# Reordering TensorE's step, and VectorE's and ScalarE's within a tile, in the first layer of a two-layer graph attention kernel

## What is computed

```python
enh = node_features + 0.1 * query_emb[None, :]
Q = (enh @ Wq + bq).reshape(N, H, D); K = ...; V = ...      # H = 4 heads of D = 64
rel = rel_w[edge_relations]                                 # 64 kinds of edge
mod_k = K[src] + 0.2 * rel[:, None, :]
scores = jnp.einsum('ehd,ehd->eh', Q[dst], mod_k) / D ** 0.5
ex = jnp.exp(scores - segment_max(scores, dst)[dst])
w = ex / segment_sum(ex, dst)[dst]
agg = segment_sum(w[:, :, None] * V[src], dst)
out = where(deg > 0, agg, V).reshape(N, H * D) @ Wo + bo
x = layernorm(out + node_features) * gamma + beta
```

## Time and profile before

| | |
|---|---|
| time, median of 3 runs | 4821.75 us (4820.29 to 4824.06) |
| the profiled execution | 4847.24 us, span 4845.9 us |
| PE busy | 4004.0 us, 83% |
| PEld busy | 2592.5 us, 53% |
| DVE busy | 3436.6 us, 71% |
| ACT busy | 2781.9 us, 57% |
| POOL busy | 3127.0 us, 65% |

### The profile page before, as it was taken

One profiled execution on the slowest core, in us unless ns is written; L12 is line 12 of the kernel. 1 busy time (PEld: TensorE's weight loads), 2 busy tenths in 40 slices (PEclk: granted clock), 3 DMA queues, 4 the chain that ended last, 5 costly groups with the idle time before them and its releaser, 6 DMA issues. The chain is left out here.

```text
span 4845.9 us, 149801 instructions
## 1 busy us (share of the span) xinstructions
PE 4004.0 (83%) x42462; PEld 2592.5 (53%) x42462; DVE 3436.6 (71%) x11602; ACT 2781.9 (57%) x7985; POOL 3127.0 (65%) x3229
## 2 busy tenths in 40 slices
PE   6978889889998888988889688777788777777785
PEld 4645545555555555555555456555565555555553
DVE  3235667677777777777777568888887787777887
ACT  2324444445454455445545367777777777777775
POOL 1226666666666666666666277777777777777773
PEclk9989999999999999999999677877767887888776
DMA  6878888888888888888888377777777777777774
GB/s 207 282 225 232 236 224 226 231 236 234 235 243 231 234 240 241 231 240 239 232 237 237 101 193 208 206 207 206 208 208 205 207 207 204 204 203 206 205 205 131
DMA packets 820558, 1052.06 MB, mean 217 GB/s; under 512 B 458633, under 2 KB 632338, under 8 KB 820464
## 3 DMA queue, kind: packets, MB, share of 16 engines
q0 software_dynamic: 225072, 726.83, 51.5%
q1 hardware_dynamic: 594078, 323.35, 26.7%
q10 hardware_dynamic: 1314, 0.99, 0.1%
HBM read 915.79 MB, written 133.39 MB: 217 GB/s over the span
## 5 line engine op out<-in xcount | busy, mean ns | idle before, releaser
L765 POOL DMA_INDIRECT typed_rows<-kv,typed_index x1563 | 1491.3, 954 | 857.4 <-PE typed_p_o L889 420.3
L1288 POOL DMA_INDIRECT plain_rows<-xp,plain_index x1563 | 1563.2, 1000 | 556.3 <-issue 437.2
L1140 ACT ACTIVATE typed_far<-typed_match,all_cst 128x416 bf16<-128x416 uint8 x521 | 334.2, 642 | 1002.2 <-DVE typed_col L991 983.8
L1393 PE MATMUL plain_p_o<-plain_rows,plain_weight_t 128*64 128x130 f32 (+1 forms) x8336 | 864.3, 350 | 49.5 <-DVE plain_weight_t L1419 48.8
L1380 PE MATMUL plain_p_s<-all_cst,plain_rows 128*128 128x128 f32 (+1 forms) x2084 | 453.9, 317 | 362.0 <-DMA plain_rows<-xp,plain_index 360.2
L1393 PEld LDWEIGHTS plain_p_o<-plain_rows,plain_weight_t 128*64 128x64 f32 (+1 forms) x8336 | 574.2, 170 | 212.0 <-issue 131.7
L851 PE MATMUL typed_p_kt<-all_cst,typed_rows 128*128 128x128 f32 x3126 | 473.8, 290 | 255.8 <-DMA typed_rows<-kv,typed_index 254.9
L964 DVE TENSOR_TENSOR typed_kt<-typed_p_kt,typed_rel 128x768 f32<-128x768 f32 x521 | 497.0, 954 | 230.7 <-PE typed_p_kt L851 202.2
L1380 PEld LDWEIGHTS plain_p_s<-all_cst,plain_rows 128*128 128x128 f32 (+1 forms) x2084 | 334.9, 173 | 515.1 <-issue 497.4
L851 PEld LDWEIGHTS typed_p_kt<-all_cst,typed_rows 128*128 128x128 f32 x3126 | 345.1, 145 | 359.1 <-DMA typed_rows<-kv,typed_index 299.0
L1426 DVE CUSTOM_DVE_ANT_0 plain_alpha<-plain_alpha,plain_far 128x416 f32<-128x416 f32 x521 | 310.6, 596 | 313.1 <-ACT plain_alpha L1542 299.9
(11 more groups left out here) (190 smaller groups left out, 6341.7 us busy)
## 6 DMA issues: line engine op xcount, KB each, us to landing
typed_match<-match SPq DMA_DIRECT2D x131, 208.0 KB
plain_match<-match SPq DMA_DIRECT2D x131, 208.0 KB
agg<-qkv_zero SPq DMA_DIRECT2D x98, 264.0 KB
typed_agg<-agg SPq DMA_DIRECT2D x98, 264.0 KB
plain_agg<-agg SPq DMA_DIRECT2D x98, 264.0 KB
kv<-qkv_kv SPq DMA_DIRECT2D x98, 258.0 KB
typed_kinds<-match SPq DMA_DIRECT2D x131, 192.0 KB
typed_rows<-kv,typed_index POOLq DMA_INDIRECT x1563
```

What stands on the lines that cost most here:

```text
L765: pool.indirect_dma_start(rows[:, r, j, :], None, k.kv, bass.IndirectOffsetOnAxis(ap=index[:, g, at:at + 1], axis=0)).then_inc(rows_in[r], 16)
L1140: act.activation(far[:], match[:, slab, t.slot(TPB)], ACT.Square, bias=cst[:, C_CODE:C_CODE + 1], scale=FAR).then_inc(far_ready, 1)
L1288: pool.indirect_dma_start(rows[:, r, j, :], None, k.xp, bass.IndirectOffsetOnAxis(ap=index[:, g, at:at + 1], axis=0)).then_inc(rows_in[r], 16)
L1393: last = pe.matmul(p_o[at:at + HC, t.slot(2), 0:2 * V], weight_t[0:e, t.slot(2), j * P + at:j * P + at + HC], val[:, 2 * V * g:2 * V * g + ...
```

## The change

TensorE's step gets another order, and VectorE's and ScalarE's lists get the same one. No instruction, wait, lag or buffer is added or removed.

- TensorE: from relations, keys, turned weights, scores, sums to turned weights, sums, scores, relations, keys. A block's update keeps its place ahead of the step, and the wait for `message_t_ready` stays with the sums, which are now second in the step.
- VectorE: from keys, weight copy, kinds, scores to weight copy, scores, kinds, keys, and the block pieces behind them as before.
- ScalarE: from message, relations, weight copy, mask, exponential, sums to message, weight copy, sums, exponential, relations, mask, and the block pieces behind them as before.

```diff
@@ attend_typed, TensorE
-            parts = (TilePart(0, relate), TilePart(KEY, arrive), TilePart(TURN_LAG, turn_weights), TilePart(SCORE, score))
-
             def step(t, copied=None):
-                for part in parts:
+                for part in (TilePart(TURN_LAG, turn_weights), TilePart(LAG, lambda b: aggregate(b, copied)), TilePart(SCORE, score),
+                             TilePart(0, relate), TilePart(KEY, arrive)):
                     part.at(t)
-                TilePart(LAG, lambda b: aggregate(b, copied)).at(t)
@@ attend_typed, VectorE
-            interleave(v, FIRST, TilePart(KEY + 2, add_keys), TilePart(TURN_LAG + 2, copy_weights), TilePart(0, prepare), TilePart(SCORE + 2, lower_bound),
+            interleave(v, FIRST, TilePart(TURN_LAG + 2, copy_weights), TilePart(SCORE + 2, lower_bound), TilePart(0, prepare), TilePart(KEY + 2, add_keys),
                        BlockPart(3, 8, end_norm), BlockPart(3, 5, normalize), BlockPart(6, 5, vary), BlockPart(4, 2, sum_up), BlockPart(5, 0, join),
@@ attend_typed, ScalarE
-            interleave(act, FIRST, BlockPart(2, 1, copy_message), TilePart(1, copy_relations), TilePart(TURN_LAG + 1, copy_weights), TilePart(SCORE, set_apart), TilePart(SCORE + 1, weigh), TilePart(LAG + 1, put),
+            interleave(act, FIRST, BlockPart(2, 1, copy_message), TilePart(TURN_LAG + 1, copy_weights), TilePart(LAG + 1, put), TilePart(SCORE + 1, weigh), TilePart(1, copy_relations), TilePart(SCORE, set_apart),
```

## The result

The changed kernel takes 4646.93 us (median), the kernel before 4822.91: a ratio of 0.9633, 95% interval 0.9617 to 0.9650. It saves 176 us where 109 were forecast (4713 us, range 4640 to 4840). One execution of the changed kernel took 5218.17 us at a granted clock of 0.625, where its others have 0.875 to 0.890, and the ratio leaves it out.

What follows compares the result with a forecast made beforehand. TensorE and POOL were taken to wait for each other through eight row buffers. Per 16 tiles 34.5 + 18.7 + 13.5 + 0.6 + 0.6 = 67.9 against 71.4 us, 109 us saved over 31.25 periods: 4713 us, range 4640 to 4840.

Steps and rivals of the forecast that it cites:

- The loop through the eight buffers: Sums free a row buffer, POOL refills it, keys need it: 9.73 us needed, 7.91 allowed; 7.5 us per period goes.
- The residue of 0.6: Row waits of TensorE left after the change, between 0 and 7.5 us per 16 tiles, taken as 0.6.
- The rival of full DMA engines: Transfers are the limit, half of row waits and clock loss stay: about 4790 to 4845 us, chance 0.20.
- The price: Scores wait for VectorE's add of the keys: 0.05 us in light steps, 0.5 to 0.8 with norm's piece and `join`.
- The update: TensorE's update adds 2.80 us to a 3.33 step; with 0.10 for the message copy, three steps of 6.23 make 18.7.
- `join` counted twice: VectorE's `join` piece sets a step of 3.91 us in each of three groups per 16 tiles.
- The other pieces: VectorE's norm and `sum_up` pieces set steps of 4.17 and 3.42 us, in each of three groups per 16 tiles.
- light steps and the extra piece: Four light steps of 3.38 us, 13.5 per 16 tiles, and extra piece L963 delaying VectorE's add, 0.6 per period.
- The message copy: In update steps only the turned weights cover it; it delays sums by 0 to 0.18 us, taken as 0.10.
- The clock rival: TensorE's holds bring stretches at 1.2 GHz, 1.50 us each, three per period: 4853 us, slower; chance 0.14.
- The rival without holds: VectorE doesn't hold the step, TensorE's 61.7 us per 16 tiles remains: 303 us saved, 4520 us; chance 0.08.

Runs made afterwards that it cites:

- refill_two_late: Changed kernel with POOL's refill of a buffer held for two more tiles' sums, on a slow chip: 6242.77 us, kernel before 6018.68, ratio 1.0368.
- relations_second: Changed kernel with all three engines reordered to turned weights, relations, sums, keys, scores, usual chip: 4600.80 us, kernel before 4821.49, ratio 0.9552.
- again_c: Changed kernel unaltered, second set of runs on a usual chip: 4643.35 us, kernel before 4821.49, ratio 0.9638.

## Why the prediction was right

**The bound was read rightly.** The loop through the eight buffers, 9.73 us needed against 7.91 allowed, was the gain: row waits went from 7.5 us per 16 tiles to 0 once 12.2 were allowed, the clock came to 1.00, and POOL's waits for the sums fell but stayed, 181.9 to 115.4. `refill_two_late`, on a slow chip, brings row waits back by this way alone. On a usual chip the row waits in 1000 us were 105.2 with a way of 7.91, 0.7 with 10.7 (`relations_second`) and 0 with 12.2. The residue of 0.6 that I took was 0. The rival of full DMA engines is refuted: they carried 9% more.

**The price was read rightly in kind and too high in size.** The sum had 67.9 per 16 tiles and measured 65.4. One period of `again_c` can be walked by the starts of the key transposes, from 1505.66 to 1571.22. A step with an update takes 5.84. The others are 3.47, 3.99, 3.44, 3.89, 3.76, 3.35, 3.75 behind the first update, 3.47, 4.01, 3.99 behind the second, and 3.72, 3.77, 3.43 behind the third, together 65.56 (the mean above is 65.4). Set against the sum, the difference comes apart so:

- *The update.* I took 2.80 from one place. That row has a wait in it. In the earlier trace rows the next update starts at 1552.56 (L902), and the kernel before goes on with

```profile
1554.98 0.33 PE L842 MATMUL typed_p_r<-typed_hit,typed_rel_a 128*128 128x384 bf16 x1
```

  which is 2.42 later; in the changed kernel it is 1557.58 - 1555.17 = 2.41. Three times 0.39 is 1.2. TensorE's own work is 60.5 per period, not 61.7. The gap before was then 10.9, of which 7.5 were row waits and 3.4, not 2.2, the rest that I had put down to the clock.
- *`join` counted twice.* In two of three groups an update follows the `join` step. The add is late there (1555.87, 1.41 behind the keys at 1554.46), but the scores that need it start at 1558.93 behind the update and don't wait. I had summed VectorE's cycle up to that add and then started the update step afresh. Two times 3.91 - 3.38 is 1.06. The one `join` step that is left takes 3.89.
- *The other pieces.* The steps with the norm's pieces take 3.99, 4.01 and 3.77, where I had 4.17. The 1.76 for them was again from one place; another in the kernel before, 1521.01 to 1522.58, has 1.57. That is 0.7 less. The steps with `sum_up` take 3.44, 3.99 and 3.43, where I had 3.42, which is 0.6 more. In the long one VectorE's maximum starts late, at 1550.97 behind 0.66 us marked issue. This comes once a period, and its cause is open.
- *The roots forgotten.* Two of the steps that I took for light hold the roots' pieces. They take 3.76 and 3.75 instead of 3.38, which is 0.75 the other way. The rows show one, where the maximum starts 0.39 late behind L348.
- The four steps left, 3.47, 3.35, 3.47 and 3.72, are 14.0, where light steps and the extra piece had 14.1.

67.9 less 0.6, 1.2, 1.06, 0.16 for the other pieces together, and 0.1, plus 0.75, is 65.5 for 65.56, so no part of it is left over. The errors mostly lay on one side, each from a place read once or a step summed twice. In the full kernel 2.5 x 31.25 = 78 us of extra gain were expected from this, and 67 were measured. That the time still fell inside the range, 7 us above its lower end, is owed to the width of the range as well: the gain was 1.6 times the forecast.

**The message copy** cost what was taken: turned weights to sums are 1558.21 - 1557.58 = 0.63 instead of 0.53.

**The clock rival** is refuted. TensorE is held before the scores 121 times in 1000 us (81 marked issue, 40 for the add) for up to 0.7 us, and the granted clock of the stretch is 1.00. By the rule of the Trainium skill on short, frequent idling ("TensorE: Matmul & The Clock Gate", section "A second HAM failure mode: psum-queue depth-cycling") the clock could have swung here. It didn't, and the measurement decides.

**The rival without holds** is refuted too: 3.9 us per 16 tiles before L874, and the order that takes them away is 43 us faster.

**What no rival named** is that the gain depends on how fast the rest of the step is. I had only looked for what the new order would do on the chip of the trace.

## What to carry to other kernels

In a pipeline whose engines follow hand-written orders, count for each buffer the way from release to next use in steps, and for each hand-over the work that lies between; moving a part trades one for the other, and the best order here gave every hand-over about the cover it needs rather than the most to one. Take a duration that enters a sum several times from several places of the trace, and look for a wait inside the stretch. And where two engines alternate as the bound, walk one whole period through both instead of adding their cycles.

## What the runs showed of the hardware

The kernel before took 4822 us in two sets of runs and 6019 to 6088 us on three other chips, its runs in one set within 0.7% of each other. An order that wins 3.6% on the one kind loses 2.2% on the other. On the slow chips TensorE stopped in the middle of groups whose code has no wait inside (104.9 us in 1000 marked issue at L874), and with half of its small matmuls the kernel was about 1% faster. The cause is open. And the label issue before a group that has a semaphore wait ahead of it can hide the releaser: at 1517.60 it stood for an add that ended 0.11 us earlier.
